# Vision tower on one core: the middle stage's work in another order on four engines

## The reference

```python
h = tok(x, gamma, beta, W, b)                         # shifted patches, normed, patch product
h = h + kernel_attn(layernorm(h), positions, scales, values, W_out)
h = h + fp8_linear(layernorm(h), weight)              # h2
y = layernorm(h)
h = h + softmax(y @ y.T / sqrt(512)) @ y              # per image: h3
y = layernorm(h)
logits = y @ router_w.T + bias                        # 64 experts
topk_p, topk_i = top_k(softmax(logits), 6); topk_p /= sum(topk_p)
shared = (silu(y @ Wg.T) * (y @ Wu.T)) @ Wd.T / 2     # two shared experts
slot = rank of a (token, expert) among those of its expert   # dropped beyond C
expert_out = (silu(x_e @ w_gate) * (x_e @ w_up)) @ w_down
h = h + shared + sum over the 6 experts of p * expert_out
```

## Time and profile before

| | us |
|---|---|
| median of 3 runs | 4639.25 (4627.1 to 4649.3) |
| the profiled execution | 4668.67, span 4666.8 |
| front, 0 to 640 | 640 |
| middle stage, 640 to 2770 | 2130; routing with attention beside it from 757 |
| expert stage, 2770 to 4666.8 | 1897 |
| busy over the span | PE 2797, PE weight loads 2117, DVE 2239, ACT 1579, POOL 2460 |

### The profile page before, as it was taken

One profiled execution on the slowest core, in us unless ns is written; L12 is line 12 of the kernel. 1 busy time (PEld: TensorE's weight loads), 2 busy tenths in 40 slices (PEclk: granted clock), 3 DMA queues, 4 the chain that ended last, 5 costly groups with the idle time before them and its releaser, 6 DMA issues. The chain is left out here.

```text
span 4666.8 us, 63125 instructions
## 1 busy us (share of the span) xinstructions
PE 2796.7 (60%) x14076; PEld 2117.4 (45%) x14077; DVE 2238.7 (48%) x7761; ACT 1579.3 (34%) x4281; POOL 2460.1 (53%) x2518
## 2 busy tenths in 40 slices
PE   5888856455545445455454336666666657677663
PEld 4777733233223222232232225655565556566563
DVE  6999965454434444344354333333333333365564
ACT  5777743232222222232222102222222222222221
POOL 5777713445544545435445535555555555565653
PEclk8999965555555555555555557777777776766676
DMA  7777711121221212211112123333333323377774
GB/s 268 248 246 245 245 32 57 61 66 63 67 63 58 63 60 64 65 58 62 61 62 66 61 57 92 94 90 91 84 84 81 84 81 84 106 228 242 237 236 166
DMA packets 401889, 522.45 MB, mean 112 GB/s; under 512 B 65596, under 2 KB 329490, under 8 KB 390514
## 3 DMA queue, kind: packets, MB, share of 16 engines
q1 hardware_dynamic: 318546, 373.60, 26.7%
q0 software_dynamic: 83232, 147.75, 9.3%
HBM read 257.02 MB, written 264.08 MB: 112 GB/s over the span
## 5 line engine op out<-in xcount | busy, mean ns | idle before, releaser
L1089 POOL DMA_INDIRECT xed<-xr,idxs x1014 | 985.9, 972 | 1098.6 <-DVE xr L1671 802.4
L1098 POOL DMA_INDIRECT ytk<-yo,idxy x1080 | 1050.8, 973 | 843.7 <-issue 792.7
L1348 PE MATMUL wide<-wdt,hT 64*128 x2160 | 469.3, 382 | 584.1 <-DVE hT L1839 558.0
L1348 PEld LDWEIGHTS wide<-wdt,hT 64*128 64x128 f32 x2160 | 402.0, 276 | 637.1 <-issue 632.2
L1830 DVE SCALAR_TENSOR_TENSOR ae<-the,bank 128x256 f32<-128x256 f32 x270 | 113.6, 421 | 800.5 <-ACT the L1479 787.7
L1263 PE MATMUL wide<-xn,e 128*128 128x128 f32 (+3 forms) x1024 | 274.9, 392 | 261.9 <-ACT e L1416 247.3
L1488 ACT ACTIVATE yo<-wide,gi 128x128 f32<-128x128 f32 x1080 | 307.3, 370 | 334.1 <-PE wide L1348 183.1
L1330 PE MATMUL bank<-wgu,xeT 128*128 x2160 | 405.4, 350 | 20.2 <-issue 11.3
L1330 PEld LDWEIGHTS bank<-wgu,xeT 128*128 128x128 f32 x2160 | 385.6, 268 | 27.8 <-issue 27.2
L1263 PEld LDWEIGHTS wide<-xn,e 128*128 128x128 f32 (+3 forms) x1024 | 156.9, 202 | 378.2 <-ACT e L1416 261.0
L1473 ACT ACTIVATE xeT<-bank 128x512 f32<-128x512 f32 x270 | 164.4, 609 | 457.2 <-remote 262.6
(11 more groups left out here) (331 smaller groups left out, 5251.8 us busy)
## 6 DMA issues: line engine op xcount, KB each, us to landing
xin<-xed SPq DMA_DIRECT2D x1080, 74.0 KB
ytk<-zeros SPq DMA_DIRECT2D x42, 1536.0 KB, 9.6
yg<-ytk SPq DMA_DIRECT2D x42, 1536.0 KB
xs<-in_xcol SPq DMA_DIRECT2D x42, 1280.0 KB, 6.7
ytk<-yo,idxy POOLq DMA_INDIRECT x1080
xed<-xr,idxs POOLq DMA_INDIRECT x1014
H<-in_ximg SPq DMA_DIRECT2D x4, 2704.0 KB, 22.2
h1d<-H SPq DMA_DIRECT2D x42, 256.0 KB, 9.5
```

What stands on the lines that cost most here:

```text
L1089: p.indirect_dma_start(xed[:, :], bass.IndirectOffsetOnAxis(ap=idxs[:, slot, j, k:k + 1], axis=0), xr[:, slot, j, :], None).then_inc(scat[ ...
L1098: p.indirect_dma_start(ytk[:, :], bass.IndirectOffsetOnAxis(ap=idxy[:, slot, j:j + 1], axis=0), yo[:, slot % ES, j, :], None)\
L1348: last = pe.matmul(eO[slot % 2][:, j * D:(j + 1) * D], hT[:, slot % 2, j, :], wdt[:, bass.ds(e, 1), :].rearrange("p o f -> p (o f)"), star ...
```

## The change

On all four engines the list of parts is put in another order, and some parts are split or work on another pair. `norm_q` takes the pair of the next step. `mix` takes the pair of the step before, and stands ahead of `count`; `scores` goes behind `shared_down`. The gate product leaves `route` and becomes `shared_gate`, first in the next routing step's list. On DVE `ffn_out` is split off its statistics (`stats_x`), and the mask off `choose` (`choices`); `quant` comes first, `choose` fourth, `attn_out` behind mask and `silu_gate`, `silu_up` behind `place`, `stats_r`, `root_r` and `norm` at the end. ACT loads its function tables explicitly in `root_r` (square root) and `ready_exp` (exponential). Three waits are added on PE, `load_h3` works out which store it needs, SP begins a step earlier and LATE goes from 5 to 4.

```diff
--- before.py
+++ after.py
@@ -1048,7 +1048,7 @@
     pS0, pS1 = bank[2], bank[3]
     pP, rA = wide[0][:, 0:512], wide[0][:, 512:1024]
     rB, rC = wide[1][:, 0:512], wide[1][:, 512:1024]
-    LATE = 5
+    LATE = 4
     FILLED = 3
     WHOLE = (0, place_of(GA, LATE) + 1, LATE)
     CUT = place_of(C1, LATE) + 1
@@ -1122,10 +1122,11 @@
             def load_h3(g, slot, rnd):
 
                 nj = tiles_of(g)
-                last = 3 * (slot // 2) + 2 + slot % 2
+                exact = isinstance(g, int)
+                last = min((TG * 128 * g + TG * 128 - 1) // (2 * T), NB - 1) if exact else 3 * (slot // 2) + 2 + slot % 2
                 for p in range(2):
-                    stored = 3 * rnd + (last - p) // 2 + 1
-                    sp.wait_ge(h3_out[p], 32 * (min(stored, NB // 2) if isinstance(stored, int) else stored))
+                    stored = (0 if exact else 3 * rnd) + (last - p) // 2 + 1
+                    after(sp, h3_out[p], 32 * stored)
                 after(sp, n["h4_r"], g - 3)
                 sp.dma_start(h3s[:, slot, 0:nj, :],
                              h3d[bass.ds(TG * 128 * g, nj * 128), :].rearrange("(p j) d -> p j d", p=128))\
@@ -1148,8 +1149,9 @@
             sp.dma_start(rbias[:, :], io["rbias"].rearrange("o e -> (o e)").partition_broadcast(128)).then_inc(n["s_ws"], 16)
             sp.wait_ge(n["s_c"], 1)
             sp.dma_start(xed[ZR:ZR + 128, :], zrow[:, :]).then_inc(n["s_zr"], 16)
-            braid(sp, 2, place_of(GR + 2, LATE) + 1, LATE,
-                  [('b', 0, load_h1), ('b', 2, load_weights), ('b', 3, store_h3), ('r', 3, halves(store_h4)), ('r', 0, load_h3)], 0, GR)
+            braid(sp, 1, place_of(GR + 2, LATE) + 1, LATE, [
+                ('b', -1, load_h1), ('b', 2, load_weights), ('b', 2, store_h3), ('r', 0, load_h3),
+                ('r', 3, halves(store_h4))], 0, GR)
 
             def load_rows(q, slot, rnd):
                 rows = entries(SP, tin, TG * q, TG, ZR)
@@ -1223,6 +1225,7 @@
             def turn_q(g, slot, rnd):
                 pe.wait_ge(n["xqb_r"], g + 1)
                 after(pe, n["xqT_r"], g)
+                after(pe, n["xnT_r"], g - 1)
                 for j in range(4):
                     last = pe.transpose(pQT[:, j * D:(j + 1) * D], xqb[:, j, :], identb[:, :])
                 last.then_inc(n["qt_done"], 1)
@@ -1237,6 +1240,8 @@
             def turn_x(g, slot, rnd):
                 pe.wait_ge(n["xn_r"], g + 1)
                 after(pe, n["xnT_r"], g)
+                pe.wait_ge(n["xqT_r"], min(g + 2, NB) if isinstance(g, int) else g + 2)
+                after(pe, n["e_r"], 2 * g)
                 for i in range(2):
                     for h, m in enumerate(HALF):
                         last = pe.transpose(pX[i][:, 128 * h:128 * h + m],
@@ -1281,7 +1286,12 @@
                     dst = rB[:, j * NE:(j + 1) * NE]
                     last = pe.matmul(dst, x4T[:, j, :], rwt[:, :], start=True, stop=True)
                 last.then_inc(n["lo_done"], 1)
+
+            def shared_gate(g, slot, rnd):
+                nj = tiles_of(g)
+                pe.wait_ge(n["x4T_r"], g + 1)
                 after(pe, n["hs_r"], g)
+                pe.wait_ge(n["s_ws"], 64)
                 pe.matmul(rC[:, 0:nj * 128], sgu[:, 0:2 * F], x4T[:, 0:nj, :].rearrange("p j d -> p (j d)"),
                           start=True, stop=True).then_inc(n["gate_done"], 1)
 
@@ -1381,9 +1391,10 @@
                     pe.matmul(rC[0:1, 0:m], ones[0:NE + 1, 0:1], itin[:, 0:m], start=(part == 0), stop=(part == PARTS - 1))\
                         .then_inc(n["late_p"], 1)
 
-            parts = [('r', 1, halves(shared_up)), ('b', 0, turn_q), ('b', 0, ffn), ('b', 1, turn_x),
-                               ('b', 1, scores), ('r', 1, halves(count)), ('r', 1, halves(shared_down)), ('b', 1, mix),
-                               ('r', 0, turn_r), ('r', 0, halves(route))]
+            parts = [
+                ('r', 1, halves(shared_gate)), ('b', 0, turn_q), ('b', 2, mix), ('r', 1, halves(count)),
+                ('r', 1, halves(shared_up)), ('b', 1, turn_x), ('b', 0, ffn), ('r', 1, halves(shared_down)),
+                ('b', 1, scores), ('r', 0, turn_r), ('r', 0, halves(route))]
             braid(pe, *WHOLE, parts, 0, GR)
             lists_early()
             lists_late()
@@ -1435,9 +1446,15 @@
                 after(a, n["rb_r"], g)
                 a.activation(sdb[:, :], mvc[:, :, 1], ACT.Sqrt, bias=c["eps_ln"][:, :]).then_inc(n["sdb_r"], 1)
 
+            def ready_exp(g, slot, rnd):
+                a.nop(nofuse=True)
+                a.preload_act_table(ACT.Exp)
+
             def root_r(g, slot, rnd):
 
                 nj = tiles_of(g)
+                a.nop(nofuse=True)
+                a.preload_act_table(ACT.Sqrt)
                 a.wait_ge(n["mvd_r"], g + 1)
                 after(a, n["rc_r"], g)
                 a.activation(sdc[:, 0:nj], mvd[:, 0:nj, 1], ACT.Sqrt, bias=c["eps_ln"][:, :]).then_inc(n["sdc_r"], 1)
@@ -1489,8 +1506,10 @@
                                         scale=gi[:, slot, j, 0:1])
                 last.then_inc(n["yo_r"], 1)
 
-            braid(a, 0, WHOLE[1], LATE, [('r', 1, halves(tanh)), ('b', 0, norm_q), ('b', 1, root_x), ('r', 0, root_r), ('b', 0, copy_q),
-                              ('b', 1, copy_x), ('r', 1, probs), ('b', 1, expo), ('r', 0, halves(copy_x4))], 0, GR)
+            norm_q(0, 0, 0)
+            braid(a, 0, WHOLE[1], LATE, [
+                ('b', 1, root_x), ('r', 1, halves(tanh)), ('r', 1, probs), ('b', 0, copy_q), ('b', -1, norm_q),
+                ('b', 1, copy_x), ('r', 0, root_r), ('b', 1, ready_exp), ('r', 0, halves(copy_x4)), ('b', 1, expo)], 0, GR)
             pipeline(a, 0, NQ, [(0, copy_xe), (1, tanh_e), (3, copy_y)], EI)
 
         @block.vector
@@ -1531,10 +1550,12 @@
             def ffn_out(g, slot, rnd):
                 v.wait_ge(n["ffn_done"], g + 1)
                 after(v, n["h3_r"], g - 1)
-                after(v, n["xn_r"], g)
                 v.scalar_tensor_tensor(h2[:, slot, :, :], pF[:, :].rearrange("p (j d) -> p j d", j=4),
                                        fscale[:, 1:2], h1s[:, slot, :, :], ALU.mult, ALU.add).then_inc(n["h2_r"], 1)
+
+            def stats_x(g, slot, rnd):
                 v.wait_ge(n["h2_r"], g + 1)
+                after(v, n["xn_r"], g)
                 stats(h2[:, slot, :, :], bstc, mvc, 4, "bnc", "mvc_r", g)
 
             def norm_x(g, slot, rnd):
@@ -1603,6 +1624,9 @@
                 after(v, n["e6_r"], g)
                 v.tensor_tensor(d6[:, 0:nj, :], t8[:, 0:nj, 2:8],
                                 top1[:, slot % 2, 0:nj].unsqueeze(2).to_broadcast([128, nj, TOPK]), ALU.add).then_inc(n["d6_r"], 1)
+
+            def choices(g, slot, rnd):
+                nj = tiles_of(g)
                 v.wait_ge(n["rep_r"], g + 1)
                 v.tensor_scalar(mask[:, 0:nj, :], lr[:, 0:nj, 0:NE], -BIG / 2, None, ALU.is_le).then_inc(n["mask_r"], 1)
 
@@ -1839,9 +1863,11 @@
                 v.tensor_copy(hT[:, slot % 2, :, :].rearrange("p j d -> p (j d)"), eH[slot % 2][0:F, :])\
                     .then_inc(n["hT_r"], 1)
 
-            order = [('b', 1, ffn_out), ('r', 1, halves(silu_gate)), ('b', 0, quant), ('r', 0, stats_r), ('b', 1, root_x),
-                     ('r', 0, root_r), ('b', 1, norm_x), ('b', 2, attn_out), ('r', 1, choose), ('r', 1, halves(silu_up)),
-                     ('r', 1, place), ('r', 1, denominator), ('r', 0, norm), ('r', 1, shared_out)]
+            order = [
+                ('b', 0, quant), ('b', 1, ffn_out), ('b', 1, stats_x), ('r', 1, choose), ('b', 1, root_x),
+                ('b', 1, norm_x), ('r', 1, choices), ('r', 1, halves(silu_gate)), ('b', 2, attn_out),
+                ('r', 1, place), ('r', 1, halves(silu_up)), ('r', 1, denominator), ('r', 0, stats_r),
+                ('r', 1, shared_out), ('r', 0, root_r), ('r', 0, norm)]
             braid(v, 0, FILLED, LATE, order, 0, GR)
             constants()
             braid(v, FILLED, CUT, LATE, order, 0, GR)
```

## The result

The changed kernel takes 4573.09 us (median of 4 runs, 4569.23 to 4599.24) against 4634.7 for the kernel before on the same chip: a ratio of 0.9874, 95% interval 0.9836 to 0.9912. It is faster by 62 us, 1.3%; forecast were 4405 us and about 230 us less. The direction was right, the size a quarter of it, and the time lies 13 us above the range of 4240 to 4560.

What follows compares the result with a forecast made beforehand. The middle stage was taken as bound by engine-to-engine waits around POOL's scatter bursts, about 34 us of each interval fixed. 19 pairs x -11.2 = -213, head -29, loops +9: -233 from 4639.25, rounded to 4405 us; range 4240 to 4560.

Steps and rivals of the forecast that it cites:

- the mask ahead of the stall in the one-step interval: On DVE, choose and mask come early and can finish in the 12 to 16 us before the stall.
- part 5: ACT's explicit table loads: 4 more a pair, 5.1 us, counted at zero; uncovered, 5 us a pair.
- part 6: Three added waits on PE: their values are made before DVE's norm_x, so counted at zero.
- part 7: SP a step later with load_h3: only the next routing group's x4 waits, zero to 2 us.
- the tail: Middle stage, work left from stall's end to next burst: 7.1 us in one-step, 21.2 us in two-step intervals before.
- One-step: Burst interval holding one step: place, silu_up and denominator partly left, 3 us; 37.8 us in all, 3.3 less.
- Two-step: Burst interval holding two steps: 13.3 us from the exponentials' release, quant assumed done; 48.4 us in all, 7.9 less.
- -13.4 for the head: Head of the middle stage: LATE 4 begins routing one step earlier, saving a step without routing, 13.4 us.
- the +9 for loops: Loops cover steps 12 to 59: two more triplets, each 4.3 us longer than straight code, +9 us.
- Little of it arrives: Rival, chance 0.17: one-step interval stays at 41, stall leftovers sit in the other's tail; 3 to 4 us a pair, 4540.
- The stall shrinks: Rival, chance 0.14: fewer pending semaphore waits let work pass during the scatter; some 36 us an interval, 4000 to 4200.
- Slower: Rival, chance 0.08: each DVE wait costs 3.5 us while work is queued, outlasting the burst; +11 a pair, 4850.

Runs made afterwards that it cites:

- e1_noload: Changed kernel without its explicit table loads, so the compiler places each load at first use: 4496.46 us, 0.9867 of the kernel before.
- e12_late5: Changed kernel with LATE back at 5, so routing begins a step later: 4523.8 us, 0.9875 of the kernel before.
- e5_control: Changed kernel, unedited, as control on the chip without the stall: 3451.46 us, 0.9808 of the kernel before.
- e3_pause12: Changed kernel, POOL waiting after 12 of a burst's 24 indirect DMAs until they have landed: 4393.12 us, 0.9634 of the kernel before.
- e7_busy6: Changed kernel, POOL clearing a scratch tile after each 6 DMAs instead of waiting, on the chip without the stall: 1.0401 of the kernel before.
- e6_pause6: Changed kernel, POOL waiting after each 6 DMAs until they have landed, on the chip without the stall: 3814.14 us, 1.0838 of the kernel before.
- e10_after: Changed kernel, unedited, timed and traced on another chip with the stall: 4528.5 us, 0.9882 of the kernel before.
- e15_busy12: Changed kernel, POOL clearing a scratch tile for 1.9 us after 12 of 24 DMAs, without waiting: 4401.78 us, 0.9693 of the kernel before.
- e19_busy12_short: Changed kernel, POOL clearing a half-width scratch tile after 12 of 24 DMAs, a gap of 0.97 us: 4538.7 us, 0.9804 of the kernel before.
- e11_extra: Changed kernel with one more DVE instruction (1.22 us) per routing step, between silu_up and denominator: 4542.56 us, 0.9919 of the kernel before.

## Why the prediction was right or wrong

**Right:** that the stage is bound by waits around POOL's bursts; that front and expert stage stay; the first burst near 730 (734.14); the mask ahead of the stall in the one-step interval; part 5, table loads at nothing (e1_noload: 0.9867 against 0.9874; part 6, the added waits, was not tried); part 7, `load_h3` does not end POOL's waits, which are all put down to L1695.

**The step that failed** is "What a new order can change is what is left to do when the stall ends, and that is the tail", with the two tails then worked out from the program order: 3 us in the one-step interval, 13.3 in the two-step one. The 34.2 us to the end of the stall hold in the changed kernel. The tail does not follow from the order alone. It is set by the wait at which DVE is caught when the signals stop coming, and the sum took DVE to be further than that:

- *One-step*, 3 us left assumed, 6.5 measured. My bounds were nothing and 5.4; the upper one was too small because `attn_out`, with a wait of its own, now stands ahead of `place`. 3.7 us x 19 = 70 us.
- *Two-step*, 13.3 us after the release assumed, 17.1 measured in the loops (13 in the straight code, where 48.2 to 48.5 us match the forecast 48.4). I let PE's chain carry the tail and hid DVE's 6.5 us behind it. In fact DVE has `attn_out` and `quant` (4.0) ahead of them and a second `attn_out` behind, 11.8 us up to `place`. I had priced `quant` as "2.7 more if not done" and chosen "done". 3.1 x 19 = 58 us.
- *The base.* The terms were taken from one pair of 97.4 us, and 19 of them summed, while the text itself gives their mean as 95.9: 1.5 x 19 = 28 us too much. The controls say more: in another trace the kernel before has a mean pair of 91.8, no longer than the changed kernel's 92.3 on that chip. How much of the -56 us is the change and how much the one trace is therefore not settled; the head's 23 to 27 us show in both pairs of traces.
- *LATE*, -13.4 for the head: 10 us of it seen there, and by the traces given back further on (e12_late5).

70 + 58 + 28 = 156 us are the difference between -213 and -56; the +9 for loops stood beside them and can't be read apart.

**The rivals.** "Little of it arrives" described the mechanism: the one-step interval stays at 41, leftovers of the stall (`quant`) sit in the other's tail; its time of 4540 was the nearest, and 0.17 too small a chance for it. "The stall shrinks" didn't happen by the change alone, but the pause shows that the stall can be cut, and the argument against it ("hardly anything was pending and DVE still stood 20 us") was about the wrong side: what counts is what POOL does. "Slower", by 3.5 us a wait, didn't happen.

**Not settled:** what the stall is. Shown are that signals between engines come late while POOL issues indirect DMAs, some 10 us after the start of a burst at the earliest, that this ends within 4 us of the burst's end or in a gap of 2 us, that POOL's rate is the same with and without it, and that one chip doesn't have it. What holds the signals back is open. One rival was not tried: in the first trace of the changed kernel 668 of some 3070 signals of the middle stage have no record of their own, in e5_control 12 of 3219, and whether the recording itself takes part could only be told by times without it. What decides where DVE is caught wasn't tried either.

A pause as in e3_pause12 is some 2.4% better than the changed kernel on a chip with the stall. On the chip without it a pause cost 1.7 us (e7_busy6) or 2.9 us (e6_pause6, the wait), so one in each of 42 bursts would be 70 to 120 us, 2 to 3.5% (worked out, not run): it is no version that beats both everywhere.

## What to carry to other kernels

Where a trace shows all engines standing at waits that are long fulfilled, don't treat the standstill as a fixed length and count the work behind it in program order: look whether the instruction or its signal is late, ask at which wait each engine is caught, and price an edit at both neighbouring places. Sum a term over the mean of the intervals, not over one that was read closely, and look at a second trace of the kernel before if the intervals in the first vary. An experiment on the engine that runs undisturbed (here two microseconds of pause on POOL) can be worth more than the whole reordering of the engines that wait. And time the same pair of kernels on a second chip before you trust where the time goes.

## What the runs showed of the hardware

- In all batches but one, waits of DVE, ACT, PE and SP hang during a run of indirect DMAs on POOL, from 10 to 16 us after its start to 34.2 us (burst of 30.3 us). What comes late is the raising of the semaphore: up to 22.8 us after PE's instruction and 7.0 us after DVE's in the trace of the changed kernel. On one chip the same program has none of it (at most 0.02 us) and takes 3451 us instead of 4528 to 4573 (e5_control; e10_after, after).
- The expert stage has it as well: 1940 to 1980 us from the 42nd burst to the end with it, 1460 without (e10_after and the first trace, e5_control).
- Within the stall SP's DMA issues are 2.8 to 4.2 us apart (kernel before, 2359 to 2374 us). A gap of 1.8 to 2.1 us in POOL's issuing lets several waits pass at once (e15_busy12, e3_pause12); one of 0.97 us lets few pass (e19_busy12_short).
- More work on an engine can shorten an interval: 1.22 us more on DVE in each routing step gave two-step intervals of 49.8 us instead of 51.1 (e11_extra), though not a faster kernel.
